# Graph layer on one core: edge rows, x and node lists handed over already laid out, a PSUM bank for each group's product

## The chip, the cores and the metric

The kernel runs on one core of one Trainium2 chip. The metric is the device time of one execution in microseconds (us), given as the median of several runs. The engines are called PE (TensorE), DVE (VectorE), ACT (ScalarE), POOL (GpSimd) and SP (SyncE); SP, ACT and POOL also issue DMAs.

## The reference

N = 3125 nodes with 128 features, E = 53125 edges sorted by destination, with 64 features each, all float32.

```python
h = jnp.concatenate([x[row], edge_attr], axis=1)            # (E, 192)
h = jax.nn.relu(_bn(h @ W1 + b1, g1, be1))                  # batch norm over the edges
s = jax.ops.segment_sum(h, col, num_segments=n)
agg = jnp.where(cnt > 0, s / jnp.maximum(cnt, 1.0), 0.0)    # cnt: edges per node
h2 = jnp.concatenate([x, agg], axis=1)                      # (N, 256)
h2 = jax.nn.relu(_bn(h2 @ W2 + b2, g2, be2))                # batch norm over the nodes
ref = jax.nn.relu(h2 @ Wl + bl)
out = _layernorm(x + ref, axis=-1)
```

## The kernel before

Edges are taken in NG = 104 groups of 512 (TILES = 4 edges on each of 128 partitions). Four groups (U) make a round, 26 rounds (NI) the edge loop. `h @ W1` is split: y = x @ W1[:128] is worked out once in the setup and stored in a table in device memory (`ytab`); an edge's first part is then a gathered row of that table, its second part a product of its 64 features with W1[128:].

**Setup.** SP loads x in rows. PE turns it in seven batches (`turn_x`, L672), DVE copies the result to `xt0` (`turned_x`, L1050), PE multiplies it with W1 (L694), ACT copies y out (L885), SP stores it (L433). ACT loads the lists of sources and destinations as rows (L879, L881); PE turns both (`turn_lists`, L657) so that `srci` (gather indices) and `loc` (destination less the group's first) have an edge per partition. POOL gathers rows of x itself for the first three groups (EARLY, L587), so that these don't wait for the table. Then POOL waits for the table (`s_tab`) and the indices (`s_idx`) and begins to gather from `ytab` (L605) with group 3.

**Edge loop.** What sets the order is the order of each engine's code, written out by hand; engines meet at semaphores. In round i, for each group q:

- SP loads the group's edge features into `ear` (L419), two buffers.
- PE turns them (L708) into `psT`, ACT copies them to `eat` (`turned`, L893), PE multiplies (`product`, L714) into `psH[q % 2]`.
- POOL gathers the y rows, four DMAs a group (`gather`, L605). Groups 0 to 2 of a round have a place of their own in `res`; group 3 goes to the one buffer `away`, part of `work`. Its gather waits until the round before has spilled it (`spilled`), squared it (`sq_ready`) and summed it (`h_summed`). POOL's order is group 3 of round i, then groups 0 to 2 of round i + 1.
- DVE adds product and gathered row (`make_h`, L1112), makes the next group's one-hot matrix (`onehot_b`, L1088) and adds to the sums of h (`sum_h`, L1119) and of its square (`sum_sq`, L1126). For group 0 the one-hot first waits for the counts of the round before (`cnt_ps`), since `hotb` is a single set.
- ACT squares h (`squares`, L914), and before that issues the spill of group 3 (L907) or the save of the one-hots (L910).
- After the four groups PE counts edges per node (`counts`, L758): 16 matmuls of ones with the one-hots into `psC[0]`, and in the same bank, in 25 of the rounds, 125 columns of W2's product with x (L761), which ACT copies out and saves in device memory (`x_product_out`, L921, L923). DVE adds the counts in the middle of the next round (`add_counts`, L1103).

ACT's order in a round is the one that matters to the prediction: `turned(i, q + 1)` comes ahead of `squares(i, q)`, and for group 3 `turned(i + 1, 0)` comes ahead of the spill:

```python
                    elif not (isinstance(i, int) and i == NI - 1):
                        turned(i + 1, 0)
                    if q == 0 and not (isinstance(i, int) and i == 0):
                        x_product_out(i - 1)
                    squares(i, q)
```

and this is what POOL waits for before a gather:

```python
                if i >= 2:
                    pool.wait_ge(h_ready, g - U + 1)
                if q == KEEP and i:
                    pool.wait_ge(spilled, 16 * i)
                    pool.wait_ge(sq_ready, g - U + 1)
                    pool.wait_ge(h_summed, g - U + 1)
                if i == NI - 1 and q == 0:
                    pool.wait_ge(cnt_ps, NT)
```

**After the loop** the batch norm's sums are folded, each group is taken again (kept in `res` or loaded back), cut at a threshold and summed by destination with matmuls (L799), and the node stage (W2, batch norm, Wl, layer norm) follows.

Of the kernel before, what the change touches and what calls it, by code (L numbers as in the profile page):

```python
# [33 lines left out]
P = 128  # L34
EPS = 1e-5
TINY = 1e-20
TILES = 4
# [9 lines left out]
def gnn_kernel(nc, x, src, dst, ea, W1, b1, g1, be1, W2, b2, g2, be2, Wl, bl, out):  # L47
    N, F = x.shape
    E, FE = ea.shape
# [3 lines left out]
    NG = (E + GROUP - 1) // GROUP  # L53
    NI = NG // U
    assert F == P and FE * 2 == P and NT * PN == N and NG == NI * U and H2 == 2
    LAST = E - (NG - 1) * GROUP
    LP = LAST // TILES
    LR = LAST - LP * TILES
    PAD = N
# [14 lines left out]
    h2x_dram = nc.dram_tensor("h2x_dram", (NT, P, H2 * PN), F32, kind="Internal").ap()  # L74
# [5 lines left out]
    with ctx:  # L80
# [17 lines left out]
        ear = work2[:, 0:2, :]  # L98
        eat = work2[:, 2:4, :]
# [23 lines left out]
        ROWS = [(0, (NG - 1) // 16 * 16), ((NG - 1) // 16 * 16, NG - 1)]  # L123
# [16 lines left out]
        xn0 = tail(NT * F)  # L140
        ysb = tail(NT * F)
        srow = tail(GROUP)
        drow = tail(GROUP)
        srowf = tail(GROUP)
# [36 lines left out]

        w2x = agg[:, 0:H2 * P]
        h2x = agg[:, H2 * P:H2 * P + H2 * PN]
        assert H2 * P + H2 * PN <= GF
        xgt = [agg[:, (1 + k) * GF:(2 + k) * GF] for k in range(2)]
        srci0 = agg[:, 3 * GF:3 * GF + EARLY * TILES].bitcast(I32).rearrange("p (g j) -> p g j", g=EARLY)
        assert NT == NI - 1 and all((i + 1) * KEEP * GF <= NI * KEEP * GF - N + i * PN for i in range(NT))
# [6 lines left out]
        psA = [psH[0], psH[1], psC[0], psC[1]]  # L194

# [7 lines left out]
        s_rowset = sem("rows_preset")  # L203
        s_rows = sem("rows_loaded")
# [8 lines left out]
        s_xps = sem("x_turned_psum")  # L213
        s_xt = sem("xt_ready")
# [3 lines left out]
        s_tab = sem("table_written")  # L218
        x_out = sem("w2_x_copied")
        x_saved = sem("w2_x_saved")  # L220
        ea_loaded = [sem(f"ea_loaded{i}") for i in range(2)]
        ea_turned = sem("ea_turned")
        eat_ready = sem("eat_ready")
        prod_ready = sem("ea_product_ready")
        gathered = [sem(f"gathered{i}") for i in range(U)]
        s_src0 = sem("first_sources_loaded")
# [172 lines left out]
        def _(sp):  # L399
            xv = x.rearrange("(p t) f -> p t f", t=NT)  # L400
            xnv = xn0[0:PN, :].rearrange("p (t f) -> p t f", t=NT)
            for k, part in enumerate(XLOADS):
                t, n = part[0][0], sum(w for _, w in part)
                for a, b in CUTS:
                    sp.dma_start(xnv[a:b, t:t + n, :], xv[a:b, t:t + n, :]).then_inc(s_x[k], 16)
# [17 lines left out]
            for q in range(2):  # L423
                load_ea(0, q)
# [10 lines left out]
            for q in range(2, U):  # L435
                load_ea(0, q)
# [4 lines left out]
            with sp.Fori(1, NI - 1) as i:  # L441
                for q in range(U):
                    load_ea(i, q)
            for q in range(U - 1):
                load_ea(NI - 1, q)

            sp.wait_ge(ea_turned, NG - 2)
            sp.wait_ge(s_tab, TAB)
            e0 = (NG - 1) * GROUP
            s = ea_loaded[1]  # L450
            sp.dma_start(ear[0:LP, 1, :],
                         ea[e0:e0 + LP * TILES, :].rearrange("(p j) f -> p (j f)", j=TILES)).then_inc(s, 16)
            sp.dma_start(ear[LP:LP + 1, 1, 0:LR * FE],
# [114 lines left out]
        def _(pool):  # L568
# [23 lines left out]
            def gather(i, q):  # L592
# [8 lines left out]
                if i == NI - 1 and q == 0:  # L601
                    pool.wait_ge(cnt_ps, NT)
# [745 lines left out]
```

## Time and profile before

| | us |
|---|---|
| median of 3 runs | 865.92 (861.46 to 869.04) |
| the profiled execution | 868.43 |
| its span, first to last instruction | 866.7 |
| setup, to POOL's first gather from the table | 34.2 |
| edge loop, first to last round's `work` gather | 668.8 |
| from there to the end | 163.7 |

The span is what the profile's stretches and instructions add up in; the time around it is 1.7 us. The mean granted TensorE clock is 0.672 of full speed.

### The profile page before, as it was taken

The page shows a single profiled execution, that of the slowest core. Times are in us where ns is not written, and L with a number is a line of the kernel's source. Part 1 is how long each engine was busy: PE and PEld are TensorE (multiplying, and loading weights), DVE is VectorE, ACT ScalarE, POOL GpSimd, SP SyncE. Part 2 cuts the span into 40 slices and gives each one's busy share as a digit, 9 for nine tenths or more (in the row PEclk, how much of TensorE's full clock was granted, in tenths as well). Part 3 has the DMA queues.
Part 4 walks back from the last instruction along what each step waited for, and adds up shares of the span by engine and source line. Part 5 has one row for each costly group of instructions (what it writes and reads, how often), then busy time and mean ns, then how long its engine had stood idle before and what let it go on. Part 6 is the DMA issues. An engine that isn't in the chain of part 4 may idle for free.

```text
span 866.7 us, 11149 instructions
## 1 busy us (share of the span) xinstructions
PE 412.7 (48%) x2281; PEld 325.3 (38%) x2281; DVE 384.1 (44%) x792; ACT 205.6 (24%) x527; POOL 448.0 (52%) x540
## 2 busy tenths in 40 slices
PE   4732443325543234433244333445322627899985
PEld 4721322213332123322133222233211417899955
DVE  3533443334433234423344333444333546577785
ACT  1211111111111011111111111111111215466656
POOL 6346655566455575555665556646556355233330
PEclk9866666565556566655666655665566656899998
DMA  6323332223232223322233222333223324577702
GB/s 159 111 73 80 94 91 79 79 73 96 86 85 83 78 83 91 89 75 76 82 94 91 79 78 70 96 88 90 79 76 85 101 56 140 166 217 223 209 1 75
DMA packets 65246, 83.93 MB, mean 97 GB/s; under 512 B 19939, under 2 KB 43924, under 8 KB 65229
## 3 DMA queue, kind: packets, MB, share of 16 engines
q1 hardware_dynamic: 39885, 39.07, 16.1%
q0 software_dynamic: 13312, 27.29, 12.6%
q10 hardware_dynamic: 12032, 17.40, 5.6%
q14 instruction: 13, 0.11, 0.1%
q8 instruction: 4, 0.07, 0.0%
HBM read 63.62 MB, written 20.08 MB: 97 GB/s over the span
## 4 chain that ended last, share of the span: by engine, by line
another core or an unknown queue 35%; PE 27%; issue 18%; DVE 7%; ACT 4%; DVEq 3%; DMA 2%; ACTq 2%; POOL 0%; SPq 0%; POOLq 0%
PE psH L714 11%; PE psH L799 5%; PE psC L799 5%; ACT work L893 3%; DVEq L1094 2%; PE psT L708 2%; ACTq L910 1%; DVE res L1112 1%; DMA hotb<-hot_dram 1%; DMA res<-in_dst 1%; DVE cnt L1103 1%; DVE res L1235 1%; DVE psS L1119 1%; ACT res L322 1%
## 5 line engine op out<-in xcount | busy, mean ns | idle before, releaser
L605 POOL DMA_INDIRECT res<-ytab,srci x300 | 287.2, 957 | 97.9 <-issue 91.1
L714 PE MATMUL psH<-w1e,work 128*128 128x256 f32 x400 | 174.5, 580 | 327.3 <-ACT work L893 279.5
L714 PEld LDWEIGHTS psH<-w1e,work 128*128 128x128 f32 x400 | 101.8, 282 | 376.1 <-ACT work L893 300.5
L605 POOL DMA_INDIRECT work<-ytab,srci x104 | 100.0, 962 | 203.4 <-DVE res L1112 147.9
L1088 DVE TENSOR_TENSOR hotb<-iota,loc 128x256 bf16<-128x256 f32 x104 | 43.9, 422 | 252.5 <-remote 251.5
L893 ACT ACTIVATE work<-psT 128x256 f32<-128x256 f32 x104 | 39.9, 383 | 382.9 <-remote 294.8
L1126 DVE TENSOR_TENSOR psX<-work,psX 128x512 f32<-128x512 f32 x104 | 72.2, 694 | 43.3 <-ACT work L914 25.8
L914 ACT ACTIVATE work<-res 128x512 f32 (+1 forms) x78 | 49.1, 630 | 175.6 <-issue 97.6
L1204 DVE TENSOR_TENSOR work<-res,psX 128x512 f32<-128x512 f32 x103 | 70.7, 688 | 29.9 <-PE psC L799 15.1
L1112 DVE TENSOR_TENSOR res<-psH,res 128x512 f32 (+1 forms) x75 | 51.5, 687 | 30.6 <-PE psH L714 21.0
L628 POOL TENSOR_TENSOR agg<-agg,srci 128x64 f32 x104 | 32.2, 309 | 63.6 <-ACT srci L975 60.9
L758 PE MATMUL psC<-hotb,onesb 128*128 128x64 bf16 x416 | 24.0, 228 | 76.8 <-issue 46.1
L799 PE MATMUL psH<-work 128*128 128x128 f32 (+1 forms) x416 | 54.1, 286 | 4.8 <-ACT srci L975 3.2
L708 PE MATMUL psT<-ident,work 128*128 128x128 f32 x200 | 55.0, 371 | 0.0
L1119 DVE TENSOR_TENSOR psS<-res,psS 128x512 f32<-128x512 f32 x78 | 53.8, 689 | 0.9 <-issue 0.4
L799 PEld LDWEIGHTS psH<-work 128*128 128x128 f32 x416 | 51.8, 203 | 5.2 <-ACT srci L975 3.3
L758 PEld LDWEIGHTS psC<-hotb,onesb 128*128 128x128 bf16 x416 | 20.2, 120 | 89.4 <-issue 55.2
L1103 DVE TENSOR_TENSOR cnt<-cnt,psC 128x64 f32 x104 | 23.1, 222 | 68.8 <-issue 58.4
L799 PE MATMUL psC<-work 128*128 128x128 f32 (+1 forms) x416 | 53.0, 283 | 0.0
L799 PEld LDWEIGHTS psC<-work 128*128 128x128 f32 x416 | 51.0, 200 | 0.0
L708 PEld LDWEIGHTS psT<-ident,work 128*128 128x128 f32 x200 | 39.9, 203 | 17.2 <-issue 10.0
L761 PE MATMUL psC<-res,agg 128*128 (+1 forms) x100 | 26.3, 408 | 0.0
(164 smaller groups left out, 394.5 us busy)
## 6 DMA issues: line engine op xcount, KB each, us to landing
work<-in_edge_attr SPq DMA_DIRECT2D x103, 128.0 KB
hot_dram<-hotb ACTq DMA_DIRECT2D x26, 256.0 KB
spill<-work ACTq DMA_DIRECT2D x26, 256.0 KB
res<-spill SPq DMA_DIRECT2D x25, 256.0 KB, 3.1
res<-ytab,srci POOLq DMA_INDIRECT x300
hotb<-hot_dram SPq DMA_DIRECT2D x13, 256.0 KB, 2.7
work<-hot_dram SPq DMA_DIRECT2D x13, 256.0 KB, 3.4
h2x_dram<-agg ACTq DMA_DIRECT2D x25, 125.0 KB
```

The lines of the kernel that those rows point to most:

```text
L605: pool.indirect_dma_start(rows[:, j * F:(j + 1) * F], None, ytab, bass.IndirectOffsetOnAxis(ap=srci[:, j, g:g + 1], axis=0)).then_inc(gath ...
L708: last = pe.transpose(psT[q % 2][:, b * P:(b + 1) * P], ear[:, q % 2, b * P:(b + 1) * P], ident[:, :])
L714: last = pe.matmul(psH[q % 2][:, b * 2 * F:(b + 1) * 2 * F], eat[:, q % 2, b * P:(b + 1) * P], w1e[:, :, :].rearrange("p a f -> p (a f)"), ...
L758: last = pe.matmul(psC[0][:, q * WIN:(q + 1) * WIN], onesb[:, :], hotb[:, q, j * WIN:(j + 1) * WIN], start=(j == 0), stop=(j == TILES - 1))
L799: last = pe.matmul(psA[q][:, 0:n], mx[:, q, j * F:(j + 1) * F], hotf[:, q, j * WIN:j * WIN + n], start=(j == 0), stop=(j == TILES - 1))
L893: act.activation(eat[:, q % 2, :], psT[q % 2][:, 0:2 * P], ACT.Copy).then_inc(eat_ready, 1)
L914: act.activation(sq[:, q % 2, :], slot(i, q), ACT.Square).then_inc(sq_ready, 1)
L1088: dve.tensor_tensor(hotb[:, q, :].rearrange("p (j w) -> p j w", j=TILES), iota[:, :].unsqueeze(1).broadcast_to([P, TILES, WIN]), loc[:, :, ...
L1112: dve.tensor_tensor(slot(i, q), psH[q % 2][:, :], slot(i, q), ALU.add).then_inc(h_ready, 1)
L1119: dve.tensor_tensor(psS[:, :], slot(i, q), psS[:, :], ALU.add).then_inc(h_summed, 1)
L1126: dve.tensor_tensor(psX[:, :], sq[:, q % 2, :], psX[:, :], ALU.add).then_inc(sq_summed, 1)
L1204: dve.tensor_tensor(tiles(mx[:, q, :]), tiles(hin), negu, ALU.max).then_inc(m_ready, 1)
```

## The change

What was prepared on the chip now comes as an input in the layout that is needed; the arrays are laid out before the launch. x comes a second time, turned (`x_turned`); sources and destinations come with an edge per partition, destinations also as rows; both are filled up to whole groups. Edge features come turned, 128 x 256 a group. With that go `turn_x`, `turned_x`, `turn_lists`, the transposes of the edge features on PE and their copies on ACT (`turned`). SP loads straight into `eat`, now four buffers.

Each of a round's four products has a bank of its own (`psP`: psH0, psH1, psT0, psC1). Counts are four matmuls of 256 columns in place of 16 of 64. W2's x product is a step of its own (`x_product`): 250 columns into psT1 after the counts of rounds 0 to 11 and 125 after round 12, 13 steps in all; ACT copies and saves it behind the squares of a next round's group 0. Its table in device memory is laid out by feature and no more by tile. POOL's wait in the last round for the last x product becomes one for step 13, from round 23 on. DVE no longer waits for that copy before it adds counts, and the small chain on gamma and beta moves ahead of the indices. In the setup, ACT loads W1 and gamma first, then the list of sources, from which the early gathers now take their indices.

```diff
+        psP = [psH[0], psH[1], psT[0], psC[1]]
...
             def load_ea(i, q):
-                if not first(i, q, 2):
-                    sp.wait_ge(ea_turned, U * i + q - 1)
-                s = ea_loaded[q % 2]
-                sp.dma_start(ear[:, q % 2, :],
-                             ea[bass.ds((i * U + q) * GROUP, GROUP), :].rearrange(
-                                 "(p j) f -> p (j f)", j=TILES)).then_inc(s, 16)
+                if not first(i, q, U):
+                    sp.wait_ge(prod_ready, U * i + q - U + 1)
+                sp.dma_start(eat[:, q, :], ea[bass.ds(i * U + q, 1), :, :].rearrange("g p e -> (g p) e")
+                             ).then_inc(ea_loaded[q], 16)
...
-                if i == NI - 1 and q == 0:
-                    pool.wait_ge(cnt_ps, NT)
+                if (i + 1) * KEEP * GF > NI * KEEP * GF - N and q == 0:
+                    pool.wait_ge(x_ps, XN + 1)
...
             def product(i, q):
                 g = U * i + q
-                pe.wait_ge(ea_loaded[q % 2], 16 * (2 * i + q // 2 + 1) if not (isinstance(i, int) and g == NG - 1)
-                           else 16 * (2 * i + q // 2 + 4))
-                if not first(i, q, 2):
-                    pe.wait_ge(eat_ready, g - 1)
+                pe.wait_ge(ea_loaded[q], 16 * (i + 1))
+                if not first(i, q, U):
+                    pe.wait_ge(h_ready, g - U + 1)
                 for b in range(2):
-                    last = pe.transpose(psT[q % 2][:, b * P:(b + 1) * P], ear[:, q % 2, b * P:(b + 1) * P], ident[:, :])
-                last.then_inc(ea_turned, 1)
-                pe.wait_ge(eat_ready, g + 1)
-                if not first(i, q, 2):
-                    pe.wait_ge(h_ready, g - 1)
-                for b in range(2):
-                    last = pe.matmul(psH[q % 2][:, b * 2 * F:(b + 1) * 2 * F], eat[:, q % 2, b * P:(b + 1) * P],
+                    last = pe.matmul(psP[q][:, b * 2 * F:(b + 1) * 2 * F], eat[:, q, b * P:(b + 1) * P],
                                      w1e[:, :, :].rearrange("p a f -> p (a f)"), start=True, stop=True)
                 last.then_inc(prod_ready, 1)
...
-                for q in range(U):
-                    for j in range(TILES):
-                        last = pe.matmul(psC[0][:, q * WIN:(q + 1) * WIN], onesb[:, :], hotb[:, q, j * WIN:(j + 1) * WIN],
-                                  start=(j == 0), stop=(j == TILES - 1))
-                for h in range(H2 if turned_out else 0):
-                    last = pe.matmul(psC[0][:, U * WIN + h * PN:U * WIN + (h + 1) * PN], w2x[:, h * P:(h + 1) * P],
-                              xt0[:, bass.ds(i * PN, PN)], start=True, stop=True)
+                for j in range(TILES):
+                    last = pe.matmul(psC[0][:, 0:U * WIN].rearrange("p (q w) -> p q w", q=U), onesb[:, :],
+                                     hotb[:, :, j * WIN:(j + 1) * WIN], start=(j == 0), stop=(j == TILES - 1))
                 last.then_inc(cnt_ps, 1)
+
+            def x_product(k, n):
+
+                if not (isinstance(k, int) and k == 0):
+                    pe.wait_ge(x_out, H2 * k)
+                for h in range(H2):
+                    last = pe.matmul(psT[1][:, h * XW:h * XW + n * NT].rearrange("o (p t) -> o p t", t=NT), w2x[:, h * P:(h + 1) * P],
+                                     xtv[:, :, bass.ds(k * XP, n)].rearrange("f t p -> f p t"), start=True, stop=True)
+                last.then_inc(x_ps, 1)
...
+            act.dma_start(srci[:, :, :], src).then_inc(s_src, 16)
+            act.dma_start(drow[0:NG, :].bitcast(I32), dst_rows).then_inc(s_rows, 16)
+            act.dma_start(dsti.bitcast(I32).rearrange("p (j g) -> p j g", j=TILES), dst).then_inc(s_rows, 16)
...
+            def edge_step(i, k=None, n=XP):
                 for q in range(U):
...
                     squares(i, q)
+                    if q == 0 and k is not None:
+                        x_product_out(k, n)
```

On PE, in the body of the edge loop, the second half of a round read before (psT holds transposes, psH products, psC0 the counts and the x product):

```order
L703 ISA
L708 MATMUL psT0<-ident,work2 128x128 x2
L710 REGISTER_ALU
L714 MATMUL psH0<-w1e,work2 128x256 x2
L708 MATMUL psT1<-ident,work2 128x128 x2
L710 REGISTER_ALU
L714 MATMUL psH1<-w1e,work2 128x256 x2
L753 ISA
L758 MATMUL psC0<-hotb,onesb 128x64 x16
L761 ISA
L761 MATMUL psC0<-res,agg 128x125 x2
```

and the loop's body now, from the x product of the round before on:

```order
L700 MATMUL psT1<-res,agg 128x250 x2
L649 ISA
L651 ISA
L653 MATMUL psH0<-w1e,work2 128x256 x2
L651 REGISTER_ALU
L653 MATMUL psH1<-w1e,work2 128x256 x2
L651 REGISTER_ALU
L653 MATMUL psT0<-w1e,work2 128x256 x2
L653 MATMUL psC1<-w1e,work2 128x256 x2
L687 REGISTER_ALU
L691 MATMUL psC0<-hotb,onesb 128x256 x4
```

The transposes between the products are gone, the four products follow each other in four banks, and the x product has moved from behind the counts' last matmul in one bank to a bank of its own ahead of the next products.

On ACT, the last third of a round in the loop's body, before (L893 is the copy of the next round's first transposes, L907 the spill):

```order
L910 DMA hot_dram<-hotb 128x1024
L914 ISA
L914 ACTIVATE work<-res 128x512
L890 ISA
L892 REGISTER_ALU
L893 ACTIVATE work<-psT 128x256
L907 ISA
L907 DMA spill<-work 128x512
L914 ACTIVATE work<-work 128x512
```

and the same place now (L841 save, L845 square, L838 spill):

```order
L841 DMA hot_dram<-hotb 128x1024
L845 ISA
L845 ACTIVATE work<-res 128x512
L838 ISA
L838 DMA spill<-work 128x512
L845 ACTIVATE work<-work 128x512
```

Nothing stands between the third group's square and the spill any more.

On ACT at the program's start, before:

```order
L873 DMA agg<-in_src 128x3x4
L874 DMA w1x<-in_L_gnn_W 128x128
L875 DMA res<-in_L_gnn_g 128x128
L879 DMA res<-in_src 96x512
L879 DMA res<-in_src 7x512
```

and now:

```order
L817 DMA w1x<-in_L_gnn_W 128x128
L818 DMA res<-in_L_gnn_g 128x128
L819 DMA srci<-in_src 128x416
L820 DMA res<-in_dst_rows 104x512
L821 DMA res<-in_dst 128x416
```

The list that the early gathers read was first and is now third, and is the whole list.

## Rows read from the trace of the kernel before

**Rows 1.** Stretch of the span: us; busy us of PE, PEld, DVE, ACT, POOL; clock; DMA
```profile
63.59:702.95 639.36, 249.08 (x1070) 173.14 (x1071) 243.92 (x487) 105.64 (x222) 367.82 (x384) 0.60 0.30 84
```

**Rows 2.** Timeline: start us, us, engine, line, operation [idle before it <- releaser]; POOL, fourth-group gathers
```profile
63.59 0.95 POOL L605 DMA_INDIRECT work<-ytab,srci  x1 [9.44 <-DMA spill<-work]
...
702.95 0.95 POOL L605 DMA_INDIRECT work<-ytab,srci  x1 [0.30 <-issue]
```

**Rows 3.** Timeline of round 10, from one fourth-group gather to the next
```profile
304.16 0.95 POOL L605 DMA_INDIRECT work<-ytab,srci  x1 [6.86 <-DVE res L1112]
...
312.74 1.03 PE L758 MATMUL psC<-hotb,onesb 128*128 128x64 bf16 x16 [3.55 <-issue]
...
314.58 0.63 PE L708 MATMUL psT<-ident,work 128*128 128x128 f32 x2
314.65 0.68 DVE L1112 TENSOR_TENSOR work<-psH,work 128x512 f32<-128x512 f32 x1
...
323.30 0.95 POOL L605 DMA_INDIRECT res<-ytab,srci  x1 [0.30 <-issue]
327.13 0.38 ACT L893 ACTIVATE work<-psT 128x256 f32<-128x256 f32 x1 [13.12 <-remote]
...
327.22 0.43 DVE L1088 TENSOR_TENSOR hotb<-iota,loc 128x256 bf16<-128x256 f32 x1 [11.89 <-remote]
327.29 0.35 ACTq L907 DMA_DIRECT2D spill<-work  x1
327.56 0.69 DVE L1119 TENSOR_TENSOR psS<-work,psS 128x512 f32<-128x512 f32 x1
...
330.90 0.95 POOL L605 DMA_INDIRECT work<-ytab,srci  x1 [6.65 <-DVE res L1112]
```

**Rows 4.** Timeline of round 24, around POOL's restart with no gather under way
```profile
685.77 1.20 PE L761 MATMUL psC<-res,agg 128*128 x4
...
687.43 0.42 DVE L1088 TENSOR_TENSOR hotb<-iota,loc 128x256 bf16<-128x256 f32 x1
...
687.74 0.95 POOL L605 DMA_INDIRECT res<-ytab,srci  x1 [6.74 <-DVE work L1112]
```

**Rows 5.** Timeline of round 0: POOL's last gather, and DVE's copy of the third product
```profile
53.20 0.95 POOL L605 DMA_INDIRECT res<-ytab,srci  x1 [0.30 <-issue]
...
56.98 0.69 DVE L1109 COPY res<-psH 128x512 f32<-128x512 f32 x1 [11.25 <-remote]
```

**Rows 6.** Timeline of the setup: gamma landed, last x gather, y on PE and ACT, first table gather
```profile
9.43 0.23 DVE L1045 TENSOR_SCALAR res<-res 128x128 f32<-128x128 f32 x1 [4.77 <-DMA res<-in_L_gnn_g]
...
18.38 0.95 POOL L587 DMA_INDIRECT res<-in_x,agg  x1 [0.30 <-issue]
...
20.92 0.60 ACT L885 ACTIVATE res<-psH 125x512 f32<-125x512 f32 x1 [6.78 <-remote]
...
27.70 1.95 PE L694 MATMUL psH<-w1x,res 128*125 128x128 f32 x8
...
31.28 0.28 ACT L885 ACTIVATE res<-psH 125x128 f32<-125x128 f32 x1 [1.00 <-PE psH L694]
...
34.18 0.95 POOL L605 DMA_INDIRECT work<-ytab,srci  x1 [14.85 <-DMA ytab<-res]
```

**Rows 7.** The page's groups: busy us, mean ns of one | idle before, releaser
```profile
L893 ACT ACTIVATE work<-psT 128x256 f32<-128x256 f32 x104 | 39.9, 383 | 382.9 <-remote 294.8
...
L1103 DVE TENSOR_TENSOR cnt<-cnt,psC 128x64 f32 x104 | 23.1, 222 | 68.8 <-issue 58.4
```

**Rows 8.** Timeline of the last round: DVE adds group 103
```profile
714.02 0.68 DVE L1112 TENSOR_TENSOR work<-psH,work 128x512 f32<-128x512 f32 x1
```

**Rows 9.** Timeline of round 20: one-hot, spill and POOL's restart
```profile
589.93 0.42 DVE L1088 TENSOR_TENSOR hotb<-iota,loc 128x256 bf16<-128x256 f32 x1 [7.77 <-remote]
...
592.76 0.35 ACTq L907 DMA_DIRECT2D spill<-work  x1
...
596.28 0.95 POOL L605 DMA_INDIRECT work<-ytab,srci  x1 [3.70 <-DMA spill<-work]
```

More of the change, by code:

```diff
@@ L179, in gnn_kernel @@
         assert H2 * N + NT * F + (H2 + H2 + 1) * P <= 9 * KEEP * GF and near <= (NI - 3) * KEEP * GF
+        XP = 10
+        XW = XP * NT
+        XN = PN // XP
+        XLAST = (PN - XN * XP) * NT
         w2x = agg[:, 0:H2 * P]
-        h2x = agg[:, H2 * P:H2 * P + H2 * PN]
-        assert H2 * P + H2 * PN <= GF
+        h2x = agg[:, 3 * GF:3 * GF + H2 * XW]
         xgt = [agg[:, (1 + k) * GF:(2 + k) * GF] for k in range(2)]
-        srci0 = agg[:, 3 * GF:3 * GF + EARLY * TILES].bitcast(I32).rearrange("p (g j) -> p g j", g=EARLY)
-        assert NT == NI - 1 and all((i + 1) * KEEP * GF <= NI * KEEP * GF - N + i * PN for i in range(NT))
+        assert H2 * XW <= 512 and XLAST and XN + 1 <= (NI * KEEP * GF - N) // (KEEP * GF) - 1
         psT = [pb(f"psT{i}", [P, 512]) for i in range(2)]
@@ L718, in turn_first @@
             def turn_first(q):
-                pe.wait_ge(ea_loaded[q % 2], 16 * (q // 2 + 1))
-                if q >= 2:
-                    pe.wait_ge(eat_ready, q - 1)
-                for b in range(2):
-                    last = pe.transpose(psT[q % 2][:, b * P:(b + 1) * P], ear[:, q % 2, b * P:(b + 1) * P], ident[:, :])
-                last.then_inc(ea_turned, 1)
                 if q < EARLY:
@@ L750, in counts @@
             def counts(i):
-                turned_out = not (isinstance(i, int) and i == NI - 1)
                 pe.wait_ge(hotb_ready, U * (i + 1))
@@ L1095, in add_counts @@
                 dve.wait_ge(cnt_ps, i + 1)
-                if not (isinstance(i, int) and i == NI - 1):
-                    dve.wait_ge(x_out, i + 1)
                 for q in range(U):
@@ L1338, with whole_groups @@
     arrays, args = {}, []
-    for name in _INS:
-        a = np.ascontiguousarray(inputs[name])
+    given = {name: np.asarray(inputs[name]) for name in _INS}
+    x, src, dst, ea = (given[name] for name in _INS[:4])
+    N, F = x.shape
+    E, FE = ea.shape
+    NT = 25
+    NG = -(-E // GROUP)
+    def whole_groups(a, fill):
+        return np.concatenate([a, np.full((NG * GROUP - E,) + a.shape[1:], fill, a.dtype)])
+    src, dst, ea = whole_groups(src, N), whole_groups(dst, N), whole_groups(ea, 0)
+    laid = {
+        'x': x,
+        'x_turned': x.reshape(N // NT, NT, F).transpose(2, 1, 0),
+        'src': src.reshape(NG, P, TILES).transpose(1, 2, 0),
+        'dst': dst.reshape(NG, P, TILES).transpose(1, 2, 0),
+        'dst_rows': dst.reshape(NG, GROUP),
+        'edge_attr': ea.reshape(NG, P, 2, 2, FE).transpose(0, 3, 4, 2, 1).reshape(NG, 2 * FE, 2 * P),
+    }
+    laid.update((name, given[name]) for name in _INS[4:])
+    for name, a in laid.items():
+        a = np.ascontiguousarray(a)
         arrays[f"in_{name}"] = a
```

221 lines of the change are left out of this document (73 added, 148 removed).

## The prediction

> **What bounds the kernel now.** I first cut the span into stages. The edge loop is 639 us of 866.7, and no engine is full in it: POOL (GpSimd) is busy for 368 us, PE for 249, DVE for 244 [rows 1]. Then I followed one engine through the loop, POOL, because its gathers carry all neighbour rows. Its gather of a round's fourth group (into `work`) starts at 63.59 in round 1 and at 702.95 in round 25 [rows 2]: 24 rounds of (702.95 - 63.59) / 24 = 26.64 us. A round holds 16 gathers; from 304.16 to the last start at 323.30 are 15 steps of 1.276 us [rows 3], nearly all 0.95 us of work and 0.30 of issue, so the 16 fill some 20.1 to 20.4 us. The other 6 are a wait. The row at 330.90 names a DVE sum for it, but the reader should see that DVE had ended that line's work long before.
>
> So I read this round in order of time. PE sends off the count matmuls at 312.74 and the transposes of the next round's first group at 314.58. ACT, which only copies these transposes, starts at 327.13, its wait called remote; DVE, whose one-hot waits for the counts, starts at 327.22 [rows 3]. PE's results are seen 12 us after their matmuls stand in the trace, 3.8 us after POOL's last gather started. With no gather under way it doesn't happen: in round 24 PE's x product ends at 686.97 and DVE goes on at 687.43 [rows 4]. I call this the hold: while gathers stream, late results of PE come out with the end of the stream. It is not tied to the count matmuls: in round 0 DVE gets a product at 56.98, again 3.8 us after the last gather's start at 53.20 [rows 5], and in the setup ACT waits 6.8 us, until 20.92, for y, with the twelfth x gather started at 18.38 [rows 6].
>
> What comes last after the hold: ACT copies the transposes (327.13), then issues the spill of `away` (327.29). The group was summed at 314.65 + 0.68, but its spill stands behind that copy on ACT. It must land before POOL may overwrite `away`: 327.29 to 330.90 is 3.61 us [rows 3].
>
> **The change part by part.**
>
> *Edge rows come transposed; PE's transposes and ACT's copies go.* 104 copies of 383 ns are 39.9 us of ACT [rows 7]; a group's two transposes are 0.63 us of PE [rows 3]. Neither engine is full, so their length is worth nothing; their place is. ACT now issues the spill when the fourth group is summed, near 315.4, and by the 3.61 us above it has landed by 319. POOL's other wait remains: DVE's sum of the fourth group (`h_summed`), which stands on DVE behind `onehot_b(i+1, 0)`, and that waits for the counts (`cnt_psum_ready`). If the hold stays, this is late next: the sum starts at 327.56 and takes 0.69, so 328.25. For the step from a last release to POOL's gather I take round 24, where PE ends at 686.97 and POOL starts at 687.74: 0.77 [rows 4]. Restart at 329.02 in place of 330.90 is 1.88 us a round; 24 rounds: 45.1 us.
>
> *A bank per product.* PE can send all four products of a round directly behind the counts, inside the earlier stream, and DVE no longer waits for PE after the hold. That lies ahead of the counts, whose result has 12 us to spare, so I take nothing. Behind a late product stand DVE's `make_h` and all after it; POOL feels it only through the fourth group, a rival below.
>
> *Four count matmuls for 16*, 1024 columns either way, 1.03 us now [rows 3]: 0 if the hold stays, since the result waits for the stream; without it, at most that 1.03. *W2's x product*, 13 steps of 250 columns for 25 of 125, reads x with a step of 125 numbers, which no row shows. Its four matmul passes take 1.20 us now [rows 4]; between no gain and four times that, it would still run in mid-stream, with the 12 us above as cover: 0, and 3.6 a step (47 in all) if that cover went. Its copies and saves on ACT halve in number and follow the squares, and DVE stops waiting for the copy before it adds counts: 0 for the same reason.
>
> *The last round.* Before, POOL had to wait in round 24 for all x products (687.74), so DVE's last round ran beside its gathers, and group 103's sum started 714.02 - 702.95 = 11.07 us after its gather [rows 2, 8]. Now the last gathers start straight after the hold, 329.02 - 327.22 = 1.8 us behind DVE's one-hot. DVE then needs a full chain: from the one-hot (26.7 before 327.22, so 300.5) to `make_h` at 314.65, 14.2; and the last round's counts come first, (23.1 + 68.8) / 26 = 3.5 [rows 7]. 17.7 - 1.8 = 15.9, of which a little is waiting for PE that goes: 15. It costs 4 (bounds 0 and 5).
>
> *The setup.* The transposes of x, their copies on DVE and the list transposes go. Best case: y runs without a break once gamma has landed (9.43, then three short operations of DVE: 10.3), in 6 batches of 2.0, plus 1.0 for bases and the last, ACT's copy 0.3 and the 2.6 from ACT's last copy to POOL's gather (31.56 to 34.18): 26.2, not 34.18: -8. Worst case: the list for the x gathers stands third on ACT's queue, behind the load that lands at 9.43 [rows 6]; they start 5 us later than before, the hold on y ends 5 us later, and the batches that are left take 8.3 and not 10.4 (4 x 1.95 [rows 6] and 0.5): +3. I take 0, nearer to the row in which the hold stands. Round 0, 63.59 - 34.18 = 29.41 [rows 2, 6], I leave as it is; without its hold it would be 20 (-9).
>
> *The last stage* reads h2x in longer pieces, under window sums that don't wait for them: 0.
>
> The sum goes against the profiled execution: its span 866.7 is 868.4 with what lies around it. -45.1 + 4 = -41.1, so 827.3. That execution is 2.5 above the median of the runs shown, 865.92: 825.
>
> One page speaks against the term that stays. The rows have PE's results late exactly while gathers stream [rows 3]. The Trainium skill ("SBUF — State Buffer", section "Who interferes with whom") says that DMA never contends with a compute engine and that PE's ports are shared with nobody. By that rule the hold would have another cause than the stream, and fewer, denser instructions might end it: the first rival's time. The trace gives no cause, only a 12 us delay for which the rule has no place.
>
> **The rivals.**
>
> *The hold goes, or mostly.* It may hang on the bunch of 22 short matmul passes (counts, x product, transposes) sent in some 2.5 us. For it: in round 20 the counts came out early, DVE at 589.93 with gathers still being issued; only ACT's copy of the transposes kept the spill until 592.76 and POOL until 596.28 [rows 9]. Against it: ACT's 294.8 us of remote waits [rows 7] are over 20 rounds' worth, round 0 and the setup hold without this bunch, and the new PE stream is as dense. DVE needs 14 to 18 us of a 20 us round, so POOL would run through: 24 x (26.64 - 20.1) = 157, and some 4 of round 0, the last round as before: 868.4 - 161 - 2.5 = 705. Half-way cases lie from 715 to 790.
>
> *The hold moves to the fourth product (slower).* PE now sends all products in one dense stretch. If those of groups 2 and 3 come out only at the end of their own round's stream, DVE's sum of the fourth group, the spill and its landing follow the hold one behind the other. Round 0 is such a round: DVE got its third product at 56.98 [rows 5], and it was 29.41 long. 24 rounds of 29.41 - 26.64 = 2.77 are +66: 866 + 66 = 932. It decides once the fourth product isn't out when POOL restarts. Against it: PE may send it off 8 us before the earlier stream ends. (If all products are held, but one stream ahead, POOL's next gathers wait for `h_ready` behind the hold, and the round is 24 to 25 long, as forecast.)
>
> *Nothing gained:* DVE's one-hot also waits for the save of the one-hots, and if that landed as late as the spill, POOL would gain nothing: 860 to 872. In this trace DVE's one-hot starts 0.1 us from ACT's copy, so the save was not last.
>
> **How the numbers follow.** Hold stays, spill uncovered: 0.53; 825, own range 800 to 850 (setup -8 to +3, round 0 down to -9, 1.5 to 2.7 us a round). Hold gone or mostly: 0.34, 705 and up to 790. Nothing gained: 0.05. Slower: 0.08. To leave out no more than 2 in 10 the range takes in the full release with the setup's gain and a little of round 0 (692) and ends at 850. A measurement of this kernel can tell about 1% from no change: faster 0.87, within 1% 0.05, slower 0.08.
>
> **What would show it.** Right: rounds of about 24.8 us between POOL's `work` gathers, each ended by DVE's sum of the fourth group and no more by a landing; the spill issued in mid-stream; DVE's one-hot still starting some 3.9 us after the last gather. The release: rounds of 20.1, POOL's waits all issue. The slower rival: `make_h` of a fourth group behind the stream's end, rounds over 27. The setup: POOL's first `work` gather near 34, not 26. The forecast is wrong at its root if the difference doesn't come from the rounds.

## The result, and the profile after

Measured beside the kernel before, the changed kernel takes 802.92 us (median of 4, 799.55 to 806.9) against 865.13 us (4 runs): ratio 0.9276, 95% interval 0.9227 to 0.9324. The forecast was 825 us, range 692 to 850. Its profiled execution took 800.44 us, its span is 798.6.

That is one half of the story. The experiments, run on three later occasions, had the kernel *before* at 696, 697 and 698 us, and where the changed kernel ran beside it again the same change was worth 1%. So this section says where 68 us of span went (866.7 to 798.6), and the next one what they were.

POOL's fourth-group gathers in the changed kernel's timeline, first, second, and that of round 25 (start us, us, engine, line, operation, idle before it and its releaser):

```profile
31.82 0.95 POOL L570 DMA_INDIRECT work<-ytab,srci  x1 [6.69 <-DMA ytab<-res]
...
56.47 0.95 POOL L570 DMA_INDIRECT work<-ytab,srci  x1 [4.83 <-DVE psS L1041]
...
635.46 0.95 POOL L570 DMA_INDIRECT work<-ytab,srci  x1 [0.87 <-DVE res L1034]
```

The stretch of 24 rounds between them, as in [rows 1]:

```profile
56.50:635.50 579.00, 157.87 (x523) 119.58 (x524) 240.02 (x483) 67.47 (x123) 367.96 (x385) 0.63 0.32 92
```

| stretch | before | after | measured | forecast |
|---|---|---|---|---|
| setup, to the first `work` gather | 34.2 | 31.8 | -2.4 | 0 |
| round 0 | 29.4 | 24.7 | -4.7 | 0 |
| rounds 1 to 24 | 639.4 | 579.0 | -60.4 | -45.1 |
| from round 25's gather to the end | 163.7 | 163.1 | -0.6 | +4 |

A round is 579.0 / 24 = 24.1 us long on the mean (forecast 24.8), but hardly one of them is: seven are 20.2 to 20.5 long, with no wait of POOL worth the name, nine are 26.3 to 29.2, the other eight between. Groups of POOL's gathers on the two pages, before and then after (busy us, mean ns of one | idle before, of it issue):

```profile
L605 POOL DMA_INDIRECT res<-ytab,srci x300 | 287.2, 957 | 97.9 <-issue 91.1
...
L605 POOL DMA_INDIRECT work<-ytab,srci x104 | 100.0, 962 | 203.4 <-DVE res L1112 147.9
```

```profile
L570 POOL DMA_INDIRECT res<-ytab,srci x300 | 286.8, 956 | 165.4 <-issue 89.6
L570 POOL DMA_INDIRECT work<-ytab,srci x104 | 100.2, 963 | 62.7 <-issue 28.0
```

Before, POOL waited ahead of the fourth group (`work`), and but once, in round 24, ahead of another (97.9 - 91.1 = 6.8 us). After, two thirds of its waiting, 165.4 - 89.6 = 75.8 us, stands ahead of the first three groups of a round (`res`), in mid-round, for `h_ready`: of its stops of over 2 us 13 end with DVE's `make_h` and stand there, and 4 end with DVE's sum and stand ahead of the fourth group. What is behind such a wait shows in the timeline of rounds 15 and 16 (round 15's `work` gather is the one at 389.76):

```profile
387.20 0.69 DVE L1041 TENSOR_TENSOR psS<-res,psS 128x512 f32<-128x512 f32 x1
...
389.76 0.95 POOL L570 DMA_INDIRECT work<-ytab,srci  x1 [0.31 <-issue]
...
403.57 0.95 POOL L570 DMA_INDIRECT res<-ytab,srci  x1 [0.30 <-issue]
407.00 0.22 DVE L1025 TENSOR_TENSOR cnt<-cnt,psC 128x64 f32 x1 [19.11 <-issue]
408.39 0.22 DVE L1025 TENSOR_TENSOR cnt<-cnt,psC 128x64 f32 x1 [1.18 <-issue]
...
410.23 0.68 DVE L1034 TENSOR_TENSOR res<-psT,res 128x512 f32 x1
...
411.18 0.95 POOL L570 DMA_INDIRECT res<-ytab,srci  x1 [6.66 <-DVE res L1034]
```

The reader should see three things. DVE stands idle for 19.11 us ahead of `add_counts`, and the releaser is "issue": no semaphore. What stands there are the four loads of the groups' bases into registers (L1018), four instructions each. Of these 16, 14 take 0.69 to 0.71 us here, most of them with a gap of 0.70 us behind, and the last starts at 406.25. In the shorter runs below DVE's idle time at this place is 2.2 us a round (56.4 us over 26). DVE comes free 3.43 us after POOL's last gather started, so this too ends with the stream. And POOL stops because `make_h` of the third group stands behind it on DVE. The changed kernel's groups of DVE say the same over the whole span, beside [rows 7]:

```profile
L1012 DVE TENSOR_TENSOR hotb<-iota,loc 128x256 bf16<-128x256 f32 x104 | 43.5, 419 | 18.7 <-issue 16.1 <-remote 1.5 <-PE psC L653 0.7
L1025 DVE TENSOR_TENSOR cnt<-cnt,psC 128x64 f32 x104 | 23.1, 222 | 197.0 <-issue 186.6 <-DVE cnt L1025 2.6
```

The one-hot hardly waits for the counts any more; the wait has gone to DVE's own issue, 58.4 us before and 186.6 after.

### The profile page after: what moved, and what is told of

It is laid out like the page before. It is cut to its first block and busy times, and to the rows that moved or that the text cites. A ratio compares the mean times of both kernels' runs of the same rounds, so it can differ in the third digit from the quotient of the medians.

```text
span 798.6 us, 9445 instructions
## 1 busy us (share of the span) xinstructions
PE 315.0 (39%) x1681; PEld 264.7 (33%) x1681; DVE 376.2 (47%) x784; ACT 166.2 (21%) x424; POOL 446.9 (56%) x538
## 5 line engine op out<-in xcount | busy, mean ns | idle before, releaser
L570 POOL DMA_INDIRECT res<-ytab,srci x300 | 286.8, 956 | 165.4 <-issue 89.6
L691 PE MATMUL psC<-hotb,onesb 128*128 128x256 bf16 x104 | 26.9, 414 | 434.2 <-DVE hotb L1012 331.7
L691 PEld LDWEIGHTS psC<-hotb,onesb 128*128 128x128 bf16 x104 | 11.2, 130 | 447.8 <-DVE hotb L1012 337.6
L845 ACT ACTIVATE work<-res 128x512 f32 (+1 forms) x78 | 49.1, 630 | 478.0 <-DVE hotb L1012 222.0
L1025 DVE TENSOR_TENSOR cnt<-cnt,psC 128x64 f32 x104 | 23.1, 222 | 197.0 <-issue 186.6
L1048 DVE TENSOR_TENSOR psX<-work,psX 128x512 f32<-128x512 f32 x104 | 72.2, 694 | 32.3 <-issue 20.1
L653 PE MATMUL psH<-w1e,work 128*128 128x256 f32 x200 | 76.7, 552 | 0.0
L1034 DVE TENSOR_TENSOR res<-psH,res 128x512 f32 (+1 forms) x50 | 34.4, 688 | 66.1 <-remote 28.4
L653 PEld LDWEIGHTS psH<-w1e,work 128*128 128x128 f32 x200 | 58.9, 302 | 15.9 <-issue 3.8
L1012 DVE TENSOR_TENSOR hotb<-iota,loc 128x256 bf16<-128x256 f32 x104 | 43.5, 419 | 18.7 <-issue 16.1
L743 PEld LDWEIGHTS psC<-work 128*128 128x128 f32 x416 | 49.1, 194 | 0.9 <-DVE work L1117 0.9
L845 ACT ACTIVATE work<-work 128x512 f32<-128x512 f32 x26 | 16.4, 629 | 67.6 <-issue 41.2
L653 PE MATMUL psT<-w1e,work 128*128 128x256 f32 x100 | 28.8, 415 | 0.0
L653 PE MATMUL psC<-w1e,work 128*128 128x256 f32 x100 | 25.8, 381 | 1.8 <-DMA work<-in_edge_attr 1.8
L700 PE MATMUL psT<-res,agg 128*128 (+2 forms) x52 | 26.0, 636 | 0.0
```

Source lines behind the costliest of these rows:

```text
L570: pool.indirect_dma_start(rows[:, j * F:(j + 1) * F], None, ytab, bass.IndirectOffsetOnAxis(ap=srci[:, j, g:g + 1], axis=0)).then_inc(gath ...
L653: last = pe.matmul(psP[q][:, b * 2 * F:(b + 1) * 2 * F], eat[:, q, b * P:(b + 1) * P], w1e[:, :, :].rearrange("p a f -> p (a f)"), start=T ...
L691: last = pe.matmul(psC[0][:, 0:U * WIN].rearrange("p (q w) -> p q w", q=U), onesb[:, :], hotb[:, :, j * WIN:(j + 1) * WIN], start=(j == 0) ...
L743: last = pe.matmul(psA[q][:, 0:n], mx[:, q, j * F:(j + 1) * F], hotf[:, q, j * WIN:j * WIN + n], start=(j == 0), stop=(j == TILES - 1))
L845: act.activation(sq[:, q % 2, :], slot(i, q), ACT.Square).then_inc(sq_ready, 1)
L1012: dve.tensor_tensor(hotb[:, q, :].rearrange("p (j w) -> p j w", j=TILES), iota[:, :].unsqueeze(1).broadcast_to([P, TILES, WIN]), loc[:, :, ...
```

## The experiments

**Parts of the change taken apart.** The first four kernels ran together. First the kernel before, with only ACT's order changed:

```diff
-                    elif not (isinstance(i, int) and i == NI - 1):
-                        turned(i + 1, 0)
...
                     squares(i, q)
+                    if q == U - 1 and not (isinstance(i, int) and i == NI - 1):
+                        turned(i + 1, 0)
```

> The kernel before, with one change on ACT: the spill and the square of the fourth group stand ahead of the copy of the next round's first transposes. Theory A (PE's late results come with the end of the gather stream, and what is last behind them is the spill): the spill's 1.88 us a round go, 24 x 1.88 = 45, so about 821, rounds of 24.8 us. Rival 1 (the spill was hidden behind another wait, such as the save of the one-hots): 866, nothing gained. Rival 2 (transposes held back by ACT's own order are what makes the delay): rounds near 20, 705 to 740.

Measured: 697.73 us; the kernel before, beside it, 695.88 (23 runs); ratio 1.0021, interval 0.9999 to 1.0044. Nothing gained, as rival 1 has it, but at a level that none of the three expected, so the run decides between none of them.

The changed kernel with two banks:

```diff
-        psP = [psH[0], psH[1], psT[0], psC[1]]
+        psP = [psH[0], psH[1], psH[0], psH[1]]
...
-                if not first(i, q, U):
-                    pe.wait_ge(h_ready, g - U + 1)
+                pe.wait_ge(h_ready, g - 1)
...
+                if q >= 2:
+                    pe.wait_ge(h_ready, q - 1)
```

> The changed kernel with two banks for the products instead of four (a product waits until the group two before it is made, as in the kernel before). Theory A: the banks are worth nothing, as predicted; 803, within 1%. Rival 1 (products sent in one dense stretch are what comes out late in every second round, and the stalls of 6.5 us come from there): stalls gone, rounds near 20.5, about 803 - 12 x 6.5 = 725. Rival 2 (the banks are what lets every second round run through, because PE is ahead): every round has a stall again, rounds of 24.8 to 26.6, 820 to 860.

Measured: 692.56 us, ratio 0.9943 (0.992 to 0.9966).

The changed kernel with sixteen matmuls for the counts:

```diff
-                for j in range(TILES):
-                    last = pe.matmul(psC[0][:, 0:U * WIN].rearrange("p (q w) -> p q w", q=U), onesb[:, :],
-                                     hotb[:, :, j * WIN:(j + 1) * WIN], start=(j == 0), stop=(j == TILES - 1))
+                for q in range(U):
+                    for j in range(TILES):
+                        last = pe.matmul(psC[0][:, q * WIN:(q + 1) * WIN], onesb[:, :], hotb[:, q, j * WIN:(j + 1) * WIN],
+                                         start=(j == 0), stop=(j == TILES - 1))
```

> The changed kernel with the counts as sixteen matmuls of 64 columns again instead of four of 256. Theory A (the end of the stream releases the result, the number of matmuls is no matter): 803, within 1%. Rival (the bunch of short matmuls makes the result late): counts late in every round, rounds of 24.8 or more, 820 to 860.

Measured: 692.58 us, ratio 0.9945 (0.9921 to 0.9969).

The changed kernel with one step of the x product on PE; the other 12 are left out, and with them the waits that count them, so the second layer reads a wrong product:

```diff
-                if not (isinstance(k, int) and k == 0):
-                    pe.wait_ge(x_out, H2 * k)
...
-                last.then_inc(x_ps, 1)
+                last.then_inc(x_ps, XN + 1)
...
             with pe.Fori(2, XN + 1) as i:
-                x_product(i - 1, XP)
                 edge_step(i)
-            x_product(XN, PN - XN * XP)
```

> The changed kernel, PE doing only the first step of W2's product with x and leaving the other 12 out; ACT copies and saves as before, so the second layer reads a wrong product. Theory A: that product ran in mid-stream under cover; 803, within 1%. Rival (its strided reads hold PE up, up to 3.6 us a step): 760 to 795, and the first 13 rounds shorter than the last 12.

Measured: 690.62 us, ratio 0.9908 (0.9874 to 0.9942).

In all four traces every round from 1 to 23 is 20.1 to 20.5 us. Banks, count matmuls and x product are worth at most half a per cent each in this state (the three ratios beside the whole change's 0.9904, below), but none of the four could decide what the parts do under the hold (the late results of PE that the prediction calls so), for there was none. The question became whether the kernel before itself had changed.

**The two kernels once more.** Unchanged, with a trace:

> The kernel before, unchanged, for its trace where the four runs above were made. There it took 696 us, not 866. Theory B (the hold on PE's results belongs to the place or the moment of a run, not to the kernel): where it is absent the rounds are 20.1 us, POOL waits for nothing but its own issue in them, and the whole is 696; where it is present, 26.6 and 866. Theory C (the hold is in the kernel, and something else made the runs above short): its rounds still show ACT's copy and DVE's one-hot starting 3.8 us after the last gather of a round.

> The changed kernel, unchanged. Theory B: without the hold its rounds are 20.1 to 20.3 us as well, and it takes 692, within half a per cent of the kernel before, since the rounds are bound by POOL's gathers in both; the gain of 63 us was made only where the hold stood. Where the hold is present: 803. Theory C (the change gains in any state): about 0.93 of the kernel before.

Measured: the kernel before 697.17 us (697.03 in the runs beside it); the changed kernel 691.78 us, ratio 0.9904, interval 0.9872 to 0.9936. Theory B holds. The kernel before, rounds 1 to 24 as in [rows 1], and the two groups of [rows 3, 7] with most of the waiting:

```profile
51.00:536.10 485.10, 278.02 (x1057) 189.29 (x1056) 238.19 (x480) 98.84 (x216) 367.07 (x384) 0.55 0.39 110
```

```profile
L1088 DVE TENSOR_TENSOR hotb<-iota,loc 128x256 bf16<-128x256 f32 x104 | 43.2, 415 | 0.3 <-DMA hot_dram<-hotb 0.3
L893 ACT ACTIVATE work<-psT 128x256 f32<-128x256 f32 x104 | 39.1, 376 | 46.3 <-PE psT L708 43.9 <-PE psT L724 2.3
```

The same program, the same amount of POOL work (367.07 us against 367.82), a round of 20.2 and not 26.64. ACT's idle time ahead of the copies is 46.3 us, not 382.9, and "remote" is gone from it. From one of its rounds:

```profile
235.72 1.03 PE L758 MATMUL psC<-hotb,onesb 128*128 128x64 bf16 x16 [2.85 <-DVE hotb L1088]
...
237.55 0.63 PE L708 MATMUL psT<-ident,work 128*128 128x128 f32 x2
238.30 0.39 ACT L893 ACTIVATE work<-psT 128x256 f32<-128x256 f32 x1 [1.31 <-PE psT L708]
...
239.41 0.41 DVE L1088 TENSOR_TENSOR hotb<-iota,loc 128x256 bf16<-128x256 f32 x1
239.66 0.34 ACTq L907 DMA_DIRECT2D spill<-work  x1
...
252.53 0.95 POOL L605 DMA_INDIRECT work<-ytab,srci  x1 [0.30 <-issue]
```

ACT copies the transposes 0.12 us after PE's 0.63 are over, with gathers going out every 1.257 us on either side; in [rows 3] it took 12. The spill is out 13 us before POOL needs it. The changed kernel in this state:

```profile
47.10:531.50 484.40, 162.54 (x528) 122.99 (x528) 238.58 (x481) 66.82 (x120) 367.34 (x385) 0.66 0.38 109
```

```profile
L1025 DVE TENSOR_TENSOR cnt<-cnt,psC 128x64 f32 x104 | 23.1, 222 | 66.9 <-issue 56.4
...
L570 POOL DMA_INDIRECT work<-ytab,srci x104 | 99.1, 953 | 31.7 <-issue 31.7
```

POOL's first gather sets the start, and its 416 gathers, in one row in which no start is more than 1.51 us after the one before, the length; PE's 115 us less work in the stretch change it by 0.7 us. Of the 5.2 us between the spans (697.2, 692.0), 3.9 lie ahead of round 1.

The results name chips 11 and 14 for these runs; that of the first comparison names none. On each occasion all runs showed the same level. Whether the hold belongs to a chip, a core or what else the machine did at that time is open; it was never met again, so it could not be tried.

One more difference goes with the hold, and it leaves a rival. The traces also record when semaphores move. The two long traces have 4561 and 3564 such records from landing DMAs and 1702 and 1474 from engines; the same two programs in the shorter state have 11758 and 11500, and 2098 and 1878, and the other traces of the experiments are as full. So "issue" as a releaser can be a missing record in the long traces. The late starts are not: in [rows 3] the counts' semaphore moves at 326.99 and the transposes' at 327.03, 0.23 and 0.10 us before DVE and ACT start, so it is PE's result that is late and not its reader. But what thins out the records may be what holds up PE and DVE: that the recording itself is part of the hold isn't excluded, as every run here has a span and a clock from the profiler.

**The start.** Run beside them:

```diff
+            act.dma_start(srci[:, :, 0:EARLY], src[:, :, 0:EARLY]).then_inc(s_src0, 16)
             act.dma_start(w1x[:, :], W1[0:F, :]).then_inc(s_w1x, 16)
             act.dma_start(gbc, g1.partition_broadcast(P)).then_inc(s_w1x, 16)
-            act.dma_start(srci[:, :, :], src).then_inc(s_src, 16)
+            act.dma_start(srci[:, :, EARLY:], src[:, :, EARLY:]).then_inc(s_src, 16)
```

> The changed kernel with the node lists of the first three groups loaded first on ACT's queue, as in the kernel before, and the rest of the list after W1 and gamma. The x gathers started 5.8 us later in the changed kernel (10.11, not 4.31). Theory B: without the hold POOL's stream is the bound from its first gather to the last, so they start at about 4.3 and the whole is up to 5.8 us shorter, 686 to 688, if the table of y is written by the time the 12 x gathers are through; rival (the table is then what POOL waits for): 690 to 692. With the hold: 797 to 803.

Measured: 690.64 us, ratio 0.9892 (0.9862 to 0.9922): 1.1 us less than the changed kernel beside it, less than the runs can tell. The trace bears out the rival:

```profile
4.68 1.17 POOL L553 DMA_INDIRECT res<-in_x,srci  x1 [2.65 <-DMA srci<-in_src]
...
24.85 0.95 POOL L571 DMA_INDIRECT work<-ytab,srci  x1 [5.17 <-DMA ytab<-res]
```

The x gathers start 6.7 us sooner than in the changed kernel's trace beside it (4.68, not 11.40), and POOL then waits 5.17 us for the table of y.

**DVE's loads of bases.**

```diff
-                bases = [dve.value_load(basei[0:1, bass.ds(U * i + q, 1)], min_val=0, max_val=N) for q in range(U)]
+                bases = [nc.values_load(basei[0:1, bass.ds(U * i + q, 1)], engines=(mybir.EngineType.DVE,), min_val=0,
+                                        max_val=N, skip_runtime_bounds_check_because="dst holds node numbers")
+                         for q in range(U)]
```

> The changed kernel with DVE's four loads of a round's bases made without the bounds check that follows each. In the first trace of the changed kernel these instructions took 0.70 us each while gathers streamed, and DVE's add of the counts started 8.4 us late. Theory B: without the hold they take 0.02 to 0.1 us, are hidden, and the time is that of the changed kernel within 0.3%. With the hold: a quarter of 16 such steps a round less, 1.4 to 2.8 us in the rounds that wait for DVE, so 770 to 795, if DVE's slow steps and not PE's late results set the rounds; 803 if PE's results do.

Measured: 689.09 us, ratio 0.9889 (0.9864 to 0.9914), 0.4% under the changed kernel (expected: within 0.3%), with intervals that overlap. DVE's issue there is halved, from 56.4 us to 27.2:

```profile
L1027 DVE TENSOR_TENSOR cnt<-cnt,psC 128x64 f32 x104 | 23.1, 222 | 37.6 <-issue 27.2
```

What this edit is worth under the hold, where the loads are what DVE stands still for, was not to be had.

**The hold built in.** Since the hold didn't come back, I made the part of it on which the forecast rests: a result of PE that comes out with the end of the stream. In the kernel before, alone and with the spill first:

```diff
                 for h in range(H2 if turned_out else 0):
+                    if h == H2 - 1 and not (isinstance(i, int) and i >= NI - 2):
+                        pe.wait_ge(gathered[EARLY - 1], 64 * (i + 1))
```

> The kernel before with the hold built in: in rounds 0 to 23 PE waits, ahead of its last matmul on x, until the last of the next round's first three groups of rows has landed (some 2.3 us after its last gather's start, by the landings in the traces). So the counts, and the transposes behind them, come out with the end of the stream wherever the kernel runs. If the chain of the prediction is right (transposes, ACT's copy, spill, its landing, POOL): POOL restarts 2.3 + 0.3 + 0.8 + 0.2 + 3.6 = 7.2 us after its last start, rounds of 15 x 1.257 + 7.2 = 26.0 us, and 697 + 24 x (26.0 - 20.2) = 836. Rival (a late result of PE is not enough to make such rounds, and something else belongs to them, such as DVE's slow steps of 0.70 us): under 780.

Measured: 856.88 us (before: 697.68), ratio 1.2288, interval 1.223 to 1.2346. Rounds of 26.67 us on the mean. Its timeline around one restart:

```profile
317.70 0.95 POOL L605 DMA_INDIRECT res<-ytab,srci  x1 [0.30 <-issue]
320.16 0.50 PEld L763 LDWEIGHTS psC<-res,agg 128*128 128x128 f32 x2 [11.29 <-DMA res<-ytab,srci]
...
321.20 0.43 DVE L1091 TENSOR_TENSOR hotb<-iota,loc 128x256 bf16<-128x256 f32 x1 [11.07 <-PE psC L763]
...
321.54 0.38 ACT L896 ACTIVATE work<-psT 128x256 f32<-128x256 f32 x1 [12.73 <-PE psT L708]
...
321.70 0.35 ACTq L910 DMA_DIRECT2D spill<-work  x1
...
325.26 0.95 POOL L605 DMA_INDIRECT work<-ytab,srci  x1 [6.60 <-DVE res L1115]
```

This is [rows 3] again, with a cause that was built in: ACT's copy 3.8 us after the last start, 0.16 to the spill, 3.56 to POOL (3.61 there). A late result of PE is enough for such rounds, then; what made PE late in the first trace it doesn't say.

> The same built-in hold, with the spill and the square of the fourth group ahead of the copy on ACT. By the prediction's term (POOL is then released by DVE's sum behind the one-hot, 1.8 us after the counts): restart 2.7 + 1.8 = 4.5 us after the last start, rounds of 23.4, 697 + 24 x 3.2 = 773, some 62 below the run with the hold alone; the term was 45 with the transposes released together with the counts. Rival (spill not last, or something as late behind it): within 10 us of the run with the hold alone.

Measured: 809.75 us (809.31 to 809.99), 47.1 below the run above. The prediction's term, 45.1, is for rounds 1 to 24, and there the two differ by 48.1: rounds of 24.67, each but the last of them ended by DVE's sum:

```profile
296.08 0.95 POOL L605 DMA_INDIRECT res<-ytab,srci  x1 [0.30 <-issue]
...
299.68 0.42 DVE L1091 TENSOR_TENSOR hotb<-iota,loc 128x256 bf16<-128x256 f32 x1 [9.01 <-PE psC L763]
300.02 0.69 DVE L1122 TENSOR_TENSOR psS<-work,psS 128x512 f32<-128x512 f32 x1
...
301.49 0.95 POOL L605 DMA_INDIRECT work<-ytab,srci  x1 [4.46 <-DVE psS L1122]
```

From the one-hot to POOL 1.81 us (forecast 1.80). Both rounds are longer than I had worked out (26.0 and 23.4), and their difference smaller (47 us in all, not 62): the one-hot starts 3.5 to 3.6 us after POOL's last start, not 2.7, and ACT's copy in the run above only 0.34 behind it. With the spill first, round 24 alone is 28.75, since POOL waits there for all x products.

The changed kernel with the same wait ahead of the last of its four count matmuls:

```diff
                 for j in range(TILES):
+                    if j == TILES - 1 and not (isinstance(i, int) and i == NI - 1):
+                        pe.wait_ge(gathered[EARLY - 1], 64 * (i + 1))
```

> The changed kernel with the same built-in hold, ahead of the last of its four matmuls for the counts: the forecast's own scene (counts late in every round, everything else free). By the prediction: as the kernel before with the hold and the spill first, rounds of 23.2 to 23.4, all alike, 692 + 24 x 3.1 = 766, up to 5 more for the last round. Rival (products sent behind the held counts make DVE late, and POOL waits for h in mid-round as in the changed kernel's first trace, every second round): rounds of 20.4 and 27 in turn.

Measured: 796.3 us (794.95 to 797.21). Rounds of 23.8 to 25.8, mean 24.19, none of 20:

```profile
286.03 0.95 POOL L570 DMA_INDIRECT res<-ytab,srci  x1 [0.30 <-issue]
288.55 0.10 PEld L693 LDWEIGHTS psC<-hotb,onesb 128*128 128x128 bf16 x1 [9.54 <-DMA res<-ytab,srci]
...
289.20 0.42 DVE L1015 TENSOR_TENSOR hotb<-iota,loc 128x256 bf16<-128x256 f32 x1 [7.98 <-PE psC L693]
...
291.01 0.95 POOL L570 DMA_INDIRECT work<-ytab,srci  x1 [4.03 <-DVE psS L1044]
```

Each of them is ended by DVE's sum of the fourth group. So late counts alone give the even rounds of the forecast, and the uneven ones of the first trace need more. DVE's slow instructions stand in that trace at the right place, but no run has them alone. Against the kernel before with the same built-in hold the changed one is at 796.3 / 856.9 = 0.929, beside 0.9276 in the first comparison. Part of that agreement is chance: rounds 1 to 24 differ by -59.5 us here and -60.4 there, setup and round 0 by -8.9 and -7.1, but the rest by +8.8 and -0.6.

**Both small edits together**, the list first and the short loads:

> A version that should beat both kernels: the changed kernel with the first lists loaded first and the four loads of bases without bounds checks. Without the hold its stream of gathers starts at 4.7 us and the bound is that stream plus the last stages: 687 to 689, 0.3 to 0.5% under the changed kernel, hardly more than can be measured. With the hold: 765 to 795, if DVE's slow steps set its long rounds.

Measured: 688.16 us, ratio 0.9859 (0.9828 to 0.9889), the lowest of all. The changed kernel's own ratio was 0.9904 (0.9872 to 0.9936); the intervals overlap and come from different occasions, so it beats the kernel before, and that it beats the changed one isn't shown.

## Why the prediction was right, and where not

The forecast said 825 us, the measurement 802.92, inside its range and in the forecast direction, and most of the difference comes from the rounds. But the mechanism that was forecast is borne out by the built-in runs and not by the pair that was forecast, and there luck had a part. Of the signs named for "right", the mean round is near (24.1, not 24.8) and the spill is issued in mid-stream in most rounds; but only 4 of POOL's stops end with DVE's sum of the fourth group, and the one-hot hardly waits for the counts.

*The place of the hold.* The prediction took the 12 us delay for a property of this chip's work: "while gathers stream, late results of PE come out with the end of the stream". That held for the trace it was read from. In the changed kernel's first trace it is nearly gone, and elsewhere it is absent: with the same stream, ACT takes up PE's result in 0.12 us in the kernel before on chip 14. The rival "hold goes", 705 us, was worked out as a state that the change might bring; it is the state of chips 11 and 14, with the change or without (691.8; 697.0 before, which I had not thought of). The rule of the Trainium skill ("SBUF — State Buffer", "Who interferes with whom") that DMA doesn't contend with a compute engine agrees with those traces: 0.12 us from PE to ACT amid gathers. It doesn't account for the delay of the first trace, and no run here shows that delay's cause.

*The spill term.* Right in mechanism and size, where PE's results are late: 45.1 forecast, 48.1 measured over the same rounds by the two built-in runs. Without the hold it is 0 (1.0021).

*The rounds as a whole.* -60.4, not -45.1: the term was too small by 15 us. The step that failed is the sentence that the counts' result "waits for the stream" in every round, with DVE's steps free. In the changed kernel the one-hot waits 18.7 us in all; in some rounds POOL ran through, and in others DVE stood still at its register loads, for up to 19 us, and the round was 26 to 29 long. I had read the trace before for PE's late results alone. DVE's own slow instructions (27 register instructions of 0.69 to 0.71 us in the first trace, 124 in the changed kernel's) I had not looked for. That short and long rounds give a mean near the forecast is chance. The 15 us can't be put down to DVE alone either: the built-in pair, with even rounds, has -59.5 over the same stretch. There 48.1 come with the spill first; of the other 11.4, 4.6 are round 24 (28.75 and 24.12), in which the changed kernel no longer waits for all x products, and the one-hot starts 3.19 us after POOL's last start on the mean, not 3.58, the built-in wait standing ahead of another matmul.

*Banks, counts, x product:* 0 each forecast. Without the hold the ratios to the kernel before are 0.9943, 0.9945 and 0.9908, beside 0.9904 for the whole change, with intervals that overlap. Under the hold untested. The x product's 13 steps take 26.0 us of PE in the first trace after, 2.0 a step for twice the columns: 0.8 over the 1.20 before, where I had bounded the extra at 3.6.

*The last round*, +4 (0 to 5): for the first pair the table has -0.6. Group 103's sum starts 12.50 us after round 25's `work` gather (11.07 before, 15 forecast), so 1.4 of the 4 are there, and the stages behind it are 2.0 shorter. In the built-in runs the stretch from round 25's gather to the end is 156.1, 159.9 with the spill first and 164.9 with the whole change: +8.8, over the bound. 5.5 of it stand ahead of group 103's sum (8.09 and 13.60), as DVE's last round no longer lies beside POOL's wait in round 24. So the mechanism exists; why the first pair has so little of it stays open.

*The setup and round 0:* 0 and 0, measured -2.4 and -4.7, inside the bounds (-8 to +3, and -9). The x gathers started at 10.11, not 4.31, as the worst case had it, and y was still sooner.

## What to carry to other kernels

If engines that should be independent release each other late, in bursts, with the releaser given as "remote" or "issue", repeat the unchanged kernel elsewhere before tuning against it: here that state cost some 170 us, and the whole change was worth 62 us in it and 5 outside. When a stall can't be had again, build its suspected core into the kernel as a wait; the difference of two such builds prices an edit, and what they don't reproduce shows what else the stall was made of. In the state that was met more often this kernel's loop is bound by POOL's row of gathers at 1.257 us each, and none of the edits tried on PE, ACT or DVE shortened its mean rounds of 20.1 to 20.3 us.

## What the runs showed that was not expected

- One program in two states, 861 to 869 us and, in the runs taken beside the experiments, 692 to 701 us, with equal busy times of POOL in the loop (367.8 and 367.1 us) and DMA at 84 and 110 GB/s.
- In the longer state not only PE's results are late: single register instructions of DVE, and in the changed kernel's trace of SP too, take 0.70 us while gathers stream. None of ACT's, PE's or POOL's do. In the same two kernels' traces in the shorter state no register instruction of any engine takes over 0.59 us. The two long traces also miss more than half of the records of landing DMAs.
- A PE that waits for a gather to land goes on about 2.5 us after that gather's start (286.03 to 288.55, 317.70 to 320.16), 0.2 us more than I had read from the landings.
